# A windowed-attention and axial-attention kernel: new preparation, and an engine order written out for the first and the last five images

## The reference, cut to what matters

```python
x = x + L0(gn(x))                    # gn: group normalisation, 32 groups of 8 channels
x = x + L1(gn(x))
# L0: roll by 4, cut into 4 windows of 64 tokens, 16 heads of 16 channels
q, k = rows / norm of rows ; logits = q @ k.T * scale + 16*sigmoid(bias table), masked
o = softmax(logits) @ v ; z = o @ Wo.T + bo
# L1: linear attention without softmax, along the columns (a = 0) and along the rows (a = 1)
y = sum over a of (q @ k.T) @ v @ w_out[a]     # computed as q @ (k.T @ v)
```

## Time and profile before

| | us |
|---|---|
| median of 3 runs | 929.75 (928.11 to 931.49) |
| span of the profiled execution, first to last instruction | 929.6 |
| PE busy in it | 846.4 (91%) |
| DVE busy | 724.5 (78%) |
| ACT busy | 661.2 (71%) |
| POOL busy | 487.3 (52%) |

### The profile page before, as it was taken

How to read it: one execution, slowest core, us unless ns; L and a number is a source line. 1 busy time by engine, 2 the same in 40 slices (tenths; PEclk the granted TensorE clock), 3 DMA queues, 4 the chain that set the end, 5 groups by cost and what they waited for, 6 DMA issues and landing times.

```text
span 929.6 us, 46004 instructions
## 1 busy us (share of the span) xinstructions
PE 846.4 (91%) x20128; PEld 664.4 (71%) x20128; DVE 724.5 (78%) x1557; ACT 661.2 (71%) x1106; POOL 487.3 (52%) x361
## 2 busy tenths in 40 slices
PE   2356999999999999999999999999999999999765
PEld 2244777788777777877777777778777777786554
DVE  4776778889888888888788888888988888886431
ACT  2435677777877877777777877777877887777541
POOL 5124555655555565565455565555565566555420
PEclk9677899999999999999999999999999999999977
DMA  6100233344444434434444334344444433433443
GB/s 172 44 12 19 54 76 64 74 82 89 90 90 89 83 78 90 81 74 86 91 81 89 82 81 82 75 89 81 88 91 88 90 78 74 80 72 73 90 85 80
DMA packets 334159, 74.04 MB, mean 80 GB/s; under 512 B 282357, under 2 KB 333447, under 8 KB 333959
## 3 DMA queue, kind: packets, MB, share of 16 engines
q1 hardware_dynamic: 333958, 71.11, 37.0%
HBM read 12.31 MB, written 8.40 MB: 22 GB/s over the span
## 4 chain that ended last, share of the span: by engine, by line
PE 80%; SPq 8%; DVE 3%; issue 3%; ACT 2%; DMA 2%; POOL 1%; POOLq 0%; DVEq 0%; ACTq 0%
PE ps L454 22%; PE ps L547 16%; PE ps L606 9%; PE ps L594 6%; PE ps L578 6%; PE ps L475 4%; SPq L404 4%; PE ps L501 3%; PE ps L595 3%; PE ps L492 3%; PE ps L511 3%; SPq L396 2%; SPq L346 2%; PE ps L640 2%; PE ps L630 1%
## 5 line engine op out<-in xcount | busy, mean ns | idle before, releaser
L909 POOL TENSOR_TENSOR kv<-kv,kv 128x1024 f16<-128x1024 f32 x64 | 136.9, 2139 | 99.2 <-ACT kv L717 96.4
L765 ACT ACTIVATE probs<-probs 128x1024 f32<-128x1024 f32 x64 | 67.8, 1059 | 101.6 <-DVE probs L1154 99.3
L594 PEld LDWEIGHTS ps<-q,gram_wide 128*128 128x128 f16 x2048 | 107.6, 97 | 13.8 <-issue 6.7
L594 PE MATMUL ps<-q,gram_wide 128*128 128x32 f16 x2048 | 111.2, 176 | 5.7 <-DMA gram_wide<-gram 4.6
L914 POOL TENSOR_TENSOR stat<-stat,small 128x2 f32<-128x2 f32 x64 | 43.0, 689 | 136.3 <-DVE stat L1067 132.4
L1093 DVE SCALAR_TENSOR_TENSOR gram<-ps,small,gram 128x512 f16<-128x512 f32 x128 | 94.4, 793 | 23.2 <-ACT gram L734 20.4
L595 PE MATMUL ps<-q,gram_wide 128*128 128x16 f16 x2048 | 110.6, 169 | 0.0
L595 PEld LDWEIGHTS ps<-q,gram_wide 128*128 128x128 f16 x2048 | 106.0, 97 | 0.4
L454 PE MATMUL ps<-xn,w_q 128*128 128x256 f16 x768 | 100.2, 283 | 6.5 <-POOL xn L909 4.5
L909 POOL TENSOR_TENSOR xn<-xn,xn 128x512 f16<-128x512 f32 x64 | 75.7, 1183 | 49.4 <-ACT xn L754 49.4
L734 ACT ACTIVATE gram<-ps,small 128x512 f16<-128x512 f32 x128 | 95.2, 816 | 7.3 <-PE ps L578 7.3
(11 more groups left out here) (120 smaller groups left out, 1951.0 us busy)
## 6 DMA issues: line engine op xcount, KB each, us to landing
gram_wide<-gram SPq DMA_DIRECT2D x256, 128.0 KB, 3.2
v_wide<-kv SPq DMA_DIRECT2D x512, 32.0 KB, 2.3
x_in<-x SPq DMA_DIRECT2D x32, 128.0 KB, 2.4
x_in<-x SPq DMA_DIRECT2D x64, 64.0 KB, 2.3
out<-y_out SPq DMA_DIRECT2D x32, 128.0 KB, 2.1
out<-y_out SPq DMA_DIRECT2D x64, 64.0 KB, 2.1
probs<-L_conv_w_qkv SPq DMA_DIRECT2D x1, 768.0 KB, 4.7
x<-L_conv_w_qkv SPq DMA_DIRECT2D x1, 768.0 KB, 6.6
```

Source lines behind the costliest of these rows:

```text
L594: pe.matmul(dst.rearrange("p (t i) -> p t i", t=2), high, q1[a][:, :, cols], start=True, stop=False)
L765: act.activation(part, part, ACT.Exp).then_inc(probs_ready[g], 1)
L909: return pool.tensor_tensor(dst, whole, high, ALU.subtract)
```

## The change

It adds a helper `placed(usual, moved)`: a bank is now a function of the image, with exceptions for images 0 to 2 and 25 to 31. `over_steps` is gone. Each engine has a list of calls written out for the first images (PE to the end of step 5, ACT and DVE to the end of step 4, POOL to the end of step 3, SP to the end of its step 6), then a loop over `step(k)` as before, then a list for the last images (from step 31; SP from step 33). The order inside the looped steps is unchanged; the waits that keep shared banks apart moved from the PE functions into `step`, so the written lists have waits of their own.

In the preparation, image 0 is loaded first, the small table weights are issued by ACT in place of SP, semaphores are split so that each weight is waited for by itself, and PE works on image 0's transposes before the weights. The bias table is masked in 8 instructions of 128 x 256 in place of 32 of 128 x 64, and these come after image 0's `scale_qk`. ACT writes a scaled copy of the axial weights (six more activations), from which POOL instead of DVE subtracts the low halves. DVE fills one of the four zeroed tensors. The loads of direction 1's axial weights come after the 16 read-backs. The vector through the output projection (`bias_through_out`) moves ahead of `scores(1)`.

```diff
-        QK_BANK, V_BANK, DEN_BANK, PV_BANK, Z_BANK, Y_BANK, YT_BANK, XT_BANK = 6, 2, 5, 1, 5, 1, 7, 5
-        S_BANK, KV_BANK, Q_BANK = (4, 6), (0, 0), (2, 0)
-        G_BANK, O_BANK, GM_BANK = (3, 3), (5, 3), (0, 2)
+        QK_BANK = placed(6, {0: 1, 1: 4})
+        V_BANK = placed(2, {0: 7, 30: 7, 31: 5})
+        DEN_BANK = placed(5, {0: 6, 1: 7, 30: 2})
+        PV_BANK = placed(1, {2: 0, 30: 2, 31: 3})
+        Z_BANK = placed(5, {1: 0, 2: 2, 31: 6})
+        Y_BANK = placed(1, {26: 5, 29: 2, 30: 5})
+        YT_BANK = placed(7, {25: 6, 26: 4})
+        XT_BANK = placed(5, {2: 3})
+        S_BANK = (placed(4, {0: 2, 1: 1, 30: 6, 31: 3}),
+                  placed(6, {2: 0, 30: 3}))
+        KV_BANK = (placed(0, {0: 3, 1: 4, 29: 6, 31: 6}),
+                  placed(0, {0: 4, 1: 3, 28: 3, 29: 3, 30: 5, 31: 4}))
+        Q_BANK = (placed(2, {0: 1, 2: 0, 28: 5, 30: 1}),
+                  placed(0, {0: 3, 2: 2, 28: 5, 29: 7, 31: 4}))
+        G_BANK = (placed(3, {0: 1, 29: 4, 30: 4, 31: 6}),
+                  placed(3, {0: 0, 27: 1, 28: 0, 30: 6, 31: 0}))
+        O_BANK = (placed(5, {27: 0, 28: 0, 29: 2, 30: 3, 31: 0}),
+                  placed(3, {27: 0, 29: 2, 30: 5}))
+        GM_BANK = (placed(0, {}),
+                  placed(2, {}))
         ZEROED = 4
 
-        stage_qkv = [probs[:, 0:6, :].rearrange("p a b -> p (a b)").rearrange("p (c n) -> p c n", c=2),
-                     x1[:, 0:3, :].rearrange("p a b -> p (a b)").rearrange("p (c n) -> p c n", c=2)]
-        stage_out = [kv32[0][:, a, :].rearrange("p (c n) -> p c n", c=2) for a in range(2)]
+        first_qkv = x1[:, 0:3, :].rearrange("p a b -> p (a b)").rearrange("p (c n) -> p c n", c=2)
+        stage_l1 = [{"q": first_qkv[:, :, 0:D], "kv": first_qkv[:, :, D:3 * D]},
+                    {"q": x1[:, 3, :].rearrange("p (c n) -> p c n", c=2), "kv": kv32[0][:]}]
+        for a in range(2):
+            stage_l1[a]["o"] = y_out[:, a]
+        W_BANK = (2, 3, 4, 6)
+        BO_BANK = 3
...
+            for dst, src in pieces(x_rows[0], x_in[:, 0]):
+                load(dst, src, x_loaded[0])
...
+            for t, (m, w) in enumerate((("q", Wq), ("k", Wk), ("v", Wv), ("o", Wo))):
+                load(stage_l0[m].rearrange("p (a n) -> p a n", a=2), w.rearrange("(a p) n -> p a n", p=P), w0_in[t])
+            for dst, src in pieces(x_rows[1], x_in[:, 1]):
+                load(dst, src, x_loaded[1])
...
+            def load_axial(a):
+                wi, wo = ((w_qkv0, w_out0), (w_qkv1, w_out1))[a]
+                wi = wi.rearrange("(a p) n -> p a n", p=P)
+                if a == 0:
+                    load(first_qkv, wi, w1_in[0])
+                else:
+                    load(stage_l1[1]["q"], wi[:, :, 0:D], w1_in[1])
+                    load(stage_l1[1]["kv"], wi[:, :, D:3 * D], w1_in[1])
+                load(stage_l1[a]["o"], wo.rearrange("(a p) n -> p a n", p=P), w1_in[a])
+
+            load_axial(0)
+
+            def write_table():
+                sp.wait_ge(table_step, 6)
+                sp.dma_start(scratch, table[:, 2, :]).then_inc(table_out, 16)
...
-            over_steps(step, 11)
+            load_image(pic[3])
+            write_table()
+            load_image(pic[2])
+            read_reaches()
+            sp.wait_ge(rows_in, 16 * 16)
+            load_axial(1)
+            load_image(pic[5])
+            spread_v_rows(0, pic[0])
+            spread_v_rows(1, pic[0])
+            load_image(pic[4])
+            spread_gram(0, pic[0])
+            load_image(pic[6])

+
+            for k in range(7, 33):
...
+            spread_gram(0, pic[27])
+            spread_v_rows(0, pic[28])
+            store_image(pic[24])
+            spread_gram(1, pic[27])
+            spread_v_rows(1, pic[28])
+            spread_gram(0, pic[28])
+            spread_gram(1, pic[28])
+            spread_v_rows(0, pic[29])
+            store_image(pic[26])
+            store_image(pic[25])
...
+            spread_gram(1, pic[30])
+            store_image(pic[27])
+            spread_gram(0, pic[31])
+            spread_gram(1, pic[31])
+            store_image(pic[28])
+            store_image(pic[29])
+            store_image(pic[30])
+            store_image(pic[31])
 
...
-                    reach(pe, o1_summed[1], earlier(img, 1))
-                else:
...
+            image_channels(pic[0])
+            table_hidden()
+            turn_weights(0)
+            pe.wait_ge(hidden_relu, 1)
+            group_means(0, pic[0])
+            turn_weights(1)
+            table_values()
+            turn_weights(2)
+            image_channels(pic[1])
+            turn_weights(3)
+            pe.wait_ge(w_lo[1], 1)
+            window_qk(pic[0])
+            group_means(0, pic[1])
+            pe.wait_ge(w_lo[2], 1)
+            window_v(pic[0])
+            window_qk(pic[1])
+            scores(pic[0])
+            pe.wait_ge(probs_ready[0], 1)
+            window_den(pic[0])
+            window_pv(pic[0])
+            bias_through_out()
+            scores(pic[1])
+            window_out(pic[0])
+            image_channels(pic[2])
+            pe.wait_ge(z_ready, 1)
+            image_channels(pic[3])
+            pe.wait_ge(biased[0], 2)
+            window_v(pic[1])
+            group_means(0, pic[2])
+            pe.wait_ge(v_ready, 2)
+            group_means(1, pic[0])
+            pe.wait_ge(probs_ready[0], 2)
+            window_pv(pic[1])
+            window_den(pic[1])
+            pe.wait_ge(den_turned, 2)
+            window_qk(pic[2])
+            window_out(pic[1])
+            axial_kv(0, pic[0])
+            window_v(pic[2])
+            axial_q(0, pic[0])
+            group_means(0, pic[3])
+            pe.wait_ge(kv_copied[0], 1)
+            axial_kv(1, pic[0])
+            pe.wait_ge(v_ready, 3)
+            group_means(1, pic[1])
+            axial_q(1, pic[0])
+            pe.wait_ge(kv_hi[1], 1)
+            scores(pic[2])
+            window_qk(pic[3])
+            pe.wait_ge(biased[1], 3)
...
+            axial_out(0, pic[29])
+            pe.wait_ge(kv_copied[1], 31)
+            gram_matmuls(0, pic[30])
+            axial_kv(0, pic[31])
+            pe.wait_ge(gram_lo[0], 31)
+            axial_kv(1, pic[31])
+            pe.wait_ge(o1_summed[0], 30)
+            axial_out(1, pic[29])
+            pe.wait_ge(kv_hi[0], 32)
+            gram_matmuls(1, pic[30])
+            axial_y(pic[28])
+            pe.wait_ge(o1_summed[1], 30)
+            axial_q(0, pic[31])
+            axial_out(0, pic[30])
+            pe.wait_ge(gram_lo[1], 31)
...
+            def load(dst, src, **kw):
+                act.dma_start(dst, src, **kw).then_inc(table_in, 16)
+
+            load(coords[:], c_coords)
+            load(w1_t[:], cpb_w1.rearrange("h c -> c h"), allow_slow_non_contiguous=True)
...
+            def axial_weights_high(a):
+
+                act.wait_ge(w1_in[a], 16 * (2 + a))
+                for m in ("q", "kv", "o"):
+                    act.activation(w_l1[a][m][:, 0], stage_l1[a][m], ACT.Copy, scale=WS)
+                    act.activation(stage_l1[a][m], stage_l1[a][m], ACT.Copy, scale=WS).then_inc(axial_scaled[a], 1)
...
+            axial_weights_high(0)
+            norm_reciprocals(pic[1])
+            probabilities(1, pic[0])
+            probabilities(0, pic[0])
+            qk_high(pic[1])
+            act.wait_ge(bo_proj, 1)
+            output_bias()
+            o_high(pic[0])
+            axial_weights_high(1)
+            window_bias(pic[0])
...
+            def axial_weights_low(a):
+
+                for t, m in enumerate(("q", "kv", "o")):
+                    pool.wait_ge(axial_scaled[a], t + 1)
+                    low(w_l1[a][m][:, 1], stage_l1[a][m], w_l1[a][m][:, 0]).then_inc(axial_lo[a], 1)
...
+            normed_low(0, pic[1])
+            qk_low(pic[0])
+            axial_weights_low(0)
+            qk_low(pic[1])
+            o_low(pic[0])
+            rstd(0, pic[2])
+            rstd(1, pic[0])
+            normed_low(0, pic[2])
+            o_low(pic[1])
+            columns_low(pic[0])
+            axial_weights_low(1)
+            normed_low(1, pic[0])
...
+            dve.memset(gram_wide[1][:].rearrange("p s q e t -> p (s q e t)").bitcast(F32), 0.0).then_inc(wide_zeroed, 1)
...
                 for w in range(NW):
-                    for pair in range(PAIRS):
-                        seen = reach_in[:, pair, :].rearrange("p (i j) -> p i j", j=REL)[:, ::-1, WIN - 1::-1]
-                        grid = "p (i j) -> p i j"
-                        last = dve.tensor_tensor(bias_mask[:, place(pair), w, :].rearrange(grid, j=WIN), seen,
-                                                 mask_in[:, w, :].rearrange(grid, j=WIN), ALU.add)
+                    for h in range(2):
+                        seen = reach_in[:, 4 * h:4 * h + 4, :].rearrange("p a (i j) -> p a i j", j=REL)[:, :, ::-1, WIN - 1::-1]
```

(57 more changed lines are left out.)

876 lines of the change are left out of this document (668 added, 208 removed).

## The result

The changed kernel takes 915.35 us (median of 4 runs, 912.03 to 918.50) against 928.95 us (4 runs, 928.11 to 931.49): ratio 0.983, 95% interval 0.981 to 0.986. Forecast was 900, with a range of 889 to 914 and a gain of 30 us; measured is a gain of 13.6. A second measurement of the same two kernels gave 915.37 and 930.68, ratio 0.983 (0.980 to 0.986). So the direction was right, the size was a little under half, and both medians lie 1.4 us above the end of the range; the profiled execution of the first measurement, 913.88 us, lies just inside it.

The account below looks back on a forecast made before the run. PE, busy for 91% of the span, was taken to bound the middle, image latency the start and SP's spreads the end. Start -21.4 and end -8 from 929.6 gave 900.2, say 900; range 889 to 914.

Parts of the forecast that it names:

- The bound of the middle: 25 looped steps of 25.93 us, 25.67 of it PE work: no order of work can shorten them; cost 0, bound -6.
- Scores(0): Start, image 0: scores start at 35.1 instead of 44.70, since its squares, norms and scaling no longer follow the table: -9.6.
- Image 1 and `window_qk(2)`: Start: scores(1) at 45.9 instead of 68.80 (-22.9), image 2's q and k at 59 instead of 77.40 (-18.4).
- the term of the start: Stretch up to the loop: reached at 134.3 instead of 155.66, -21.4, with ends at -10 and -30.
- image 2's term: Start: 17 us from image 2's q and k to its scores, scores(2) at 76.5, -17.2.
- POOL and DVE block each other: Rival, start: `mask_k(0)` waits for a POOL subtraction, at most 2.13 us, and all behind shifts: 902; chance 0.07.
- Image 3's term: Start: latency from q and k to scores grows from 16.3 to 19.5 us; scores(3) at 97.5 instead of 118.86, -21.4.
- Only image 0 gains: Rival, start: the 25 us cycle returns with image 2, so the time is 916; chance 0.09.
- The start packs better: Rival, start: scores(2) and (3) come at the pace of PE, giving 892; chance 0.13.
- The end: Last images: SP's chain of spreads sets the end, bound -13.1; 5 us of waits left, so -8.
- the end doesn't move: Rival, last images: one of SP's written waits takes the place of the old ones, giving 908; chance 0.20.
- Slower: Rival, middle: each looped step can wait for SP if the loop starts late; 933 at 1.3 us a step; chance 0.04.

Follow-up runs that it names:

- experiment 7: Changed kernel with the low halves of q and k of images 0 to 2 formed by DVE before the masks instead of by POOL: 915.81 us, ratio 0.984.
- experiment 2: Changed kernel with POOL's low halves of direction 1's axial weights moved directly behind image 0's o: 909.91 us, ratio 0.977.
- experiment 4: Changed kernel without its written end, direction 1's axial low halves earlier on POOL, stores of images 24 to 31 issued by ACT: 909.38 us, ratio 0.976.
- experiment 5: Changed kernel without its written end and with direction 1's axial low halves earlier on POOL, stores left on SP: 910.56 us, ratio 0.979.
- experiment 8: Changed kernel, written end kept, with the stores of images 24 to 31 issued by ACT instead of SP: 914.24 us, ratio 0.983.
- experiment 6: Changed kernel with DVE's sum y of image 26 put ahead of image 31's norm in the written end: 911.7 us, ratio 0.979.

## Why the prediction was right or wrong

**The bound of the middle** held: 25.9 us a step before and 25.8 after. The 3.6 us by which the middle is shorter were not forecast. 3.2 of them are one step of the kernel before, here beside the step ahead of it, in which PE idled 2.1 us and ran at 0.94:

```profile
412.50:438.30 25.80, 25.71 (x631) 20.39 (x631) 22.11 (x47) 20.29 (x35) 14.83 (x12) 1.00 0.41 86
```

```profile
438.30:467.30 29.00, 26.90 (x629) 21.11 (x628) 22.12 (x47) 20.76 (x35) 15.27 (x13) 0.94 0.40 86
```

No such step came in the thirteen traces after it, whose middles took 641.0 to 644.5 and whose longest step is 26.8. There is one trace of the kernel before, so whether such a step is common in it, or was chance, isn't known.

**Scores(0)**: forecast 35.1, came 32.9. The larger cause is the table's way through DRAM:

```profile
16.32 0.35 SPq L404 DMA_DIRECT2D position_table<-table x1
18.34 5.76 SPq L412 DMA_DIRECT2D gram<-position_table x16
```

The read-backs landed at 26.1, 9.8 us after the write and not 13.2. The first of them is issued 2.0 us after the write; before, the write itself took 5.84 us. I wrote that nothing there is changed, but the loads that stood around the write are ordered anew. That these made the difference isn't shown. The smaller cause the trace of before had in it. The table's first sum took 2.03 us there, and takes 0.26 now. In before POOL was clearing memory beside it; in after a POOL subtraction begins at the same time, and it is POOL that takes longer (1.29 for 1.15). I took 4.0 us for the table's arithmetic from a held row; it takes 2.2, but begins at 14.1 instead of 12.6, so the write comes only 0.6 us earlier than forecast. Against both the masks took 4.70 instead of 2.8, which experiment 7 shows to be a hold.

**Image 1 and `window_qk(2)`**: forecast 45.9 and 59, came 44.05 and 56.69. These steps stand.

**Images 2 and 3** are where the term of the start was mis-sized: -16.3 for -21.4. (The recorded sum has a slip of its own: 59 + 17 is 76.0, not 76.5.) The missing 5.1 us add up as 2.3 won up to `window_qk(2)`, 3.2 lost from there to scores(2) (against the 17.5 that 76.5 stands for), 3.9 from scores(2) to scores(3), and 0.3 behind. Two terms failed, then: the 17 us from q and k of image 2 to its scores, which measured 20.7, and the 19.5 us of image 3, from 78.61 to 102.27, which measured 23.7.

In image 2's term stands what I had as the rival "POOL and DVE block each other", right as a mechanism and placed wrongly. I priced it at one place, `mask_k(0)`, with at most 2.13 us; there it took 0.96 in all, and in its stead the masks, the sums x of images 1 and 2 and five small statistics were held. I also wrote that the second three low halves of the axial weights stand only before `normed_low(1, 0)`, as if a POOL instruction could delay nothing but POOL's queue. Experiment 2 shows that they delayed DVE by 2.95 us. The term itself goes from 20.7 to 22.3 us in the five traces with the changed kernel's start to 18.5, 20.4 and 18.6 in experiments 2, 4 and 5. But `window_qk(2)` comes about 1 us later there, since the sums of image 0 are held instead. How much of the missing 5.1 us is due to holds isn't settled by the runs: 1.8 to 3.2 us is what the start of experiment 2 got back against the two traces of the changed kernel, less than the spread of equal starts allows to tell, and three other removals got back nothing clear of it, since PE's order or a new hold took the gain. PE's clock from scores(0) to scores(2) was 0.79, but 0.74 over the same images before, so it is no new loss over the whole of them. From `window_qk(2)` to scores(2) alone it was 0.84 against 0.92 before, and what that cost isn't shown.

Image 3's term is ACT's queue. Its squares stand behind o of image 2, in after and in before:

```profile
87.55 0.63 ACT L1110 ACTIVATE o<-o 128x512 f16<-128x512 f32 x1 [0.68 <-DVE o L1705]
88.09 1.00 ACT L1075 ACTIVATE qk_sq<-ps 128x1024 f32<-128x1024 f32 x1
```

```profile
104.10 1.02 ACT L772 ACTIVATE qk_sq<-ps 128x1024 f32<-128x1024 f32 x1
```

They begin 9.5 us after `window_qk(3)`, where before it was 2.8: q and k came earlier, and the squares still waited for image 2's softmax. The prediction named this order and priced it at 3.2 us; it cost 6.7. From scores(2) to scores(3) it took 23.5 to 24.9 us in all thirteen traces since the change, with the holds moved or not. No experiment moved these squares, so this is read from the timelines and not tested. I took the latency from rows of before, though not what a queue does when two images' work stands closer together in it.

Two of the rivals are answered here. *Only image 0 gains* said 916, nearest to the 915.35 measured, but by luck: scores(1) came 24.8 us earlier. Its reason, that the 25 us cycle returns, holds for image 3 (24.9 us) and not for image 2. *The start packs better* (892) didn't come.

**The part behind scores(3)** held: forecast 36.8 us, measured 37.05, of which PE is busy 36.74.

**The end** was wrong in sign: -8 forecast, +2.4 measured; over all nine traces with the written end it takes 126.4 to 130.2 us, over the four with the usual order 125.3 to 126.2. The step that failed is that SP's chain of spreads alone sets it, and that less waiting in this chain makes the end shorter by 8. What held is the last part: from the last gram spread to the end of the span it takes 19.0 to 20.4 us in all fourteen traces (forecast 19.8). Waits of SP in the changed kernel, from 770 us on:

```profile
SPq L429 <- DVE gram L1622: 14.2, 5, 6.3
SPq L445 <- ACT y_out L1135: 10.4, 2, 7.9
SPq L439 <- POOL kv L1381: 6.1, 3, 2.7
```

SP waits 30.7 us in these three lines, and its last gram spread is issued 119.7 us after v(27) instead of 116.7 (forecast 102). That is beyond the 115 us which I had named as a sign of a wrong forecast. The last stretch before it, though, has almost no wait in it:

```profile
868.59 11.68 SPq L439 DMA_DIRECT2D v_wide<-kv x16
880.61 2.87 SPq L429 DMA_DIRECT2D gram_wide<-gram x4
883.52 2.88 SPq L445 DMA_DIRECT2D out<-y_out x3
886.45 6.56 SPq L429 DMA_DIRECT2D gram_wide<-gram x8
```

Behind v of image 31 stand image 30's second gram, a store and image 31's grams, 12.7 us up to the end of the last spread. In the usual order it was a store and image 31's grams, 8.7 us. V of image 31 is out 0.9 us earlier, the last part is 0.7 us shorter, and that makes the 2.4 us by SP's own times. But the order of SP isn't the whole of it: in experiment 8 the store is gone from between them, and the same 12.7 us remain, now with 12 spreads in them that wait for the grams. The chain of work that ended last tells the same. It runs through SP's issues for about 40 us of the end in the kernel before and for about 30 in the changed one, but for only 4 in experiment 4, whose end is as long as before. So SP's queue and the way through PE, ACT and DVE are about equally long. Experiments 4 and 8 took the stores from SP, four of them ahead of the last spread, and the end moved by at most 1.3 us. A queue that ends close to the end looks like the only bound when one adds up its own issue times.

What the rival "the end doesn't move" said of the time was right to 2.4 us. Its reason was a written wait of SP such as a store's, and experiment 8 speaks against that. Which order would shorten both ways isn't known; none tried here took the end below 125.3 us. The wait for y, 2 us of PE's time, isn't the cause of the 2.4 either, since experiment 6 showed that it only moves.

**Slower**: the loop didn't start late against SP, steps take 25.8 us, the longest 26.4.

## What to carry to other kernels

Before moving an elementwise operation to POOL, list what DVE does at that time: an instruction of 0.2 us can cost 2, and all that is queued behind it is late too. A duration read from a trace is one with its neighbours, so compare it with the shortest of its kind before it goes into a sum. When an early stage is made faster, look for what the next one's first instruction stands behind in its queue. And whether a queue is the only bound is shown by taking work from it, not by adding up what it issues: a second path of nearly the same length doesn't show in such a sum.

## What the runs showed that I had not expected

A hold that is removed comes up at the next pair: in experiments 2 and 7 the freed instruction fell from 3.71 to 0.76 and from 4.70 to 2.77, and a later one rose by 1.24 and by 0.7. The smallest DVE instructions suffer most in proportion, 2.10 for 0.17.

Runs with the same start differ in it by up to 3 us, for more than one reason. Experiment 8, the latest of the five starts, is 1.6 us behind the first trace already at scores(0). There the table's first sum was held by POOL's subtraction of xn; in the other twelve traces since the change it took 0.25 or 0.26:

```profile
14.15 1.27 DVE L1528 TENSOR_SCALAR table<-table 16x225 f32<-16x225 f32 x1
```

So a hold can be there in one execution and not in the next. The traces also differ in the places where PE's clock is at 1.2 GHz. 12 matmuls of `axial_kv(1)` for image 0 took 2.76 us at 1.00 in experiment 2, and 5.30 us at 0.50 in the changed kernel, where PE had stood idle twice just before (1.66 and 0.97 us):

```profile
69.40:74.90 5.50, 5.30 (x12) 1.65 (x12) 5.33 (x10) 3.15 (x8) 4.81 (x3) 0.50 0.07 18
```

A late input costs twice here: the idle time itself, and then matmuls at half the clock.
